# Attention kernel: row-max products in groups of two pairs over four PSUM banks, a unit's output joined in one bank, new order of jobs

## What is computed

```python
x = x + attn(layernorm(x))      # 16 heads of 64: q, k, v = x @ W.T
#   sim = q @ k.T * scale; e = exp(sim - max(sim)); out = (e / (sum(e) + 1e-10)) @ v; out @ Wo.T + bo
x = x + ffn(layernorm(x))       # blocks of 16 are rounded to an FP4 grid ahead of each product:
#   h = silu(x @ w_gate.T) * (x @ w_up.T); h @ w_down.T     (hidden width 352)
```

## Time and profile before

| | us |
|---|---|
| median of 3 runs (1461.32 to 1464.38) | 1464.04 |
| the profiled execution's own time | 1464.06 |
| its span | 1462.2 |
| TensorE busy | 1380.1 (94%) |
| VectorE, ScalarE, GpSimd busy | 1101.9 (75%), 1137.5 (78%), 1245.4 (85%) |

### The profile page before, as it was taken

How to read it: one execution, slowest core, us unless ns; L and a number is a source line. 1 busy time by engine, 2 the same in 40 slices (tenths; PEclk the granted TensorE clock), 3 DMA queues, 4 the chain that set the end, 5 groups by cost and what they waited for, 6 DMA issues and landing times.

```text
span 1462.2 us, 35256 instructions
## 1 busy us (share of the span) xinstructions
PE 1380.1 (94%) x13828; PEld 892.1 (61%) x13828; DVE 1101.9 (75%) x1717; ACT 1137.5 (78%) x2413; POOL 1245.4 (85%) x1391
## 2 busy tenths in 40 slices
PE   4899999998999999999999999999999999999965
PEld 2466665665666666666666666666666666666644
DVE  7767677677678878787887868788786878878567
ACT  3798888976888878788887878888787878878822
POOL 5798989987998988898898889899888989989932
PEclk8999999999999999999999999999999999999958
DMA  7111111111111102112111211211121121112000
GB/s 175 45 45 45 45 36 32 35 33 44 45 45 34 38 23 49 45 45 49 34 38 23 48 45 44 49 38 34 24 48 45 45 49 40 32 23 49 2 4 15
DMA packets 46660, 59.77 MB, mean 41 GB/s; under 512 B 8672, under 2 KB 21920, under 8 KB 46496
## 3 DMA queue, kind: packets, MB, share of 16 engines
q1 hardware_dynamic: 46336, 57.26, 16.8%
q10 hardware_dynamic: 160, 0.26, 0.1%
HBM read 4.80 MB, written 2.10 MB: 5 GB/s over the span
## 4 chain that ended last, share of the span: by engine, by line
PE 65%; DVE 20%; POOL 6%; ACT 5%; issue 3%; DMA 1%; SPq 0%; DVEq 0%
PE ob L635 16%; PE st L606 12%; PE st L608 10%; PE sm L587 8%; DVE negm L941 7%; POOL p_low L450 5%; PE mb L523 4%; PE mb L539 4%; PE mb L528 2%; PE mb L1242 2%; PE mb L534 2%; ACT probs L761 1%; DVE v L909 1%; DVE qv L1115 1%; DVE hidden L1119 1%
## 5 line engine op out<-in xcount | busy, mean ns | idle before, releaser
L450 POOL TENSOR_TENSOR p_low<-probs 128x512 f16<-128x512 f32 x1024 | 1083.0, 1076 | 148.2 <-ACT probs L761 145.1
L761 ACT ACTIVATE probs<-st,lift,exp_scale 128x512 f32<-128x512 f32 x1024 | 792.2, 779 | 172.4 <-PE st L608 159.9
L941 DVE TENSOR_REDUCE negm<-sm 128x1 f32<-128x1024 f32 x508 | 617.6, 1216 | 105.4 <-PE sm L587 104.2
L606 PE MATMUL st<-q_hl,k_hh 128*128 128x512 f16 x1024 | 394.7, 385 | 2.3 <-DMA q_hm<-m_low 2.3
L608 PE MATMUL st<-q_hm,k_l 128*128 128x512 f16 x1024 | 389.4, 380 | 0.0
L635 PEld LDWEIGHTS ob<-v,probs 128*128 128x128 bf16 x4096 | 279.3, 98 | 123.1 <-ACT oscl L775 1.0
L635 PE MATMUL ob<-v,probs 128*128 128x129 f16 x4096 | 322.4, 222 | 0.6 <-ACT oscl L775 0.5
L635 PEld LDWEIGHTS ob<-v,p_low 128*128 128x128 f16 x4096 | 195.7, 98 | 127.7 <-POOL p_low L450 8.7
L587 PE MATMUL sm<-k_hh,q_hl 64*128 64x512 f16 x508 | 197.5, 389 | 23.1 <-DVE negm L941 23.0
L635 PE MATMUL ob<-v,p_low 128*128 128x65 f16 x4096 | 211.2, 195 | 5.4 <-POOL p_low L450 5.3
L587 PE MATMUL sm<-k_hh,q_hm 64*128 64x512 f16 x508 | 197.7, 389 | 0.0
(11 more groups left out here) (175 smaller groups left out, 1539.1 us busy)
## 6 DMA issues: line engine op xcount, KB each, us to landing
k_hh<-k_high SPq DMA_DIRECT2D x128, 128.0 KB, 2.4
k_l<-k_low SPq DMA_DIRECT2D x64, 128.0 KB, 2.3
q_hl<-q_high SPq DMA_DIRECT2D x64, 128.0 KB, 2.3
q_hl<-q_low SPq DMA_DIRECT2D x64, 128.0 KB, 2.4
q_hm<-q_high SPq DMA_DIRECT2D x62, 128.0 KB, 2.3
x<-x SPq DMA_DIRECT2D x4, 512.0 KB, 7.3
q_hm<-m_high SPq DMA_DIRECT2D x128, 1.0 KB
q_hm<-m_low SPq DMA_DIRECT2D x128, 1.0 KB
```

The source lines that it names most:

```text
L450: return pool.tensor_tensor(p_low[b][:, j, :], p, p.bitcast(BF16)[:, 1::2], ALU.subtract)
L606: pe.matmul(st[s % 2][:, :], k_hh[n][:, s * P:(s + 1) * P], q_hl[n][:, half * HALF:(half + 1) * HALF], start=True, stop=False)
L761: nc.scalar.activation(probs[k % 2][:, s, :], st[s % 2][:, :], ACT.Exp, bias=lift[:, 0:1], scale=exp_scale[:, head, pair:pair + 1]).then_i ...
L941: nc.vector.tensor_reduce(negm[k % 2][:, s // 2:s // 2 + 1], banks[:, :, :].rearrange("p a n -> p (a n)"), AX.X, ALU.max, negate=True).the ...
```

## The change

`scores` is called in slots 0 and 4 and makes two pairs in a row: four matmuls in four banks. `sm` has four banks; its upper two serve jobs as well, as X0 and X1, beside one bank MB that only jobs use. A job in X0 or X1 waits until VectorE has reduced the group's first pair, and a group waits until the jobs ahead of it in X0 and X1 have been taken. VectorE reduces the first pair in slot 0 or 4 and the second in slot 1 or 5.

A unit's output (4 tiles x 65 columns) lies in the single bank `ob`. The high part is multiplied twice with the same probabilities, by 65 columns and by 64 that are added to the same place, so `join` on GpSimd falls away. The order within a unit is `VALUES`. ScalarE copies 260 columns out in slot 0 (`out_taken`), VectorE makes sums and reciprocals, and ScalarE scales 4 x 64 columns from SBUF in slots 3 and 4. `JOBS` has a new order. In the round ahead, `turn_rest` moves from slot (1, 1) to (3, 2), with the high and low parts behind it, and v0 waits for them; the DMA that ScalarE issues there moves from (1, 2) to (1, 3).

```diff
--- before.py
+++ after.py
...
...
-VC = 1 + 2 * DH
-VL = 1 + DH
-OT = 256
+VC = 1 + DH
...
-JOBS = [("k0", 0, (0, 1), (0, 2), (0, 2)), ("m", 1, (0, 1), (0, 2), (0, 2)), ("k1", 1, (0, 3), (0, 4), (0, 4)),
-        ("q0", 0, (0, 5), (0, 6), (0, 6)), ("t0", 0, (0, 7), (1, 0), None), ("m", 0, (1, 1), (1, 2), (1, 2)),
-        ("q1", 1, (1, 1), (1, 2), (1, 2)), ("o0", 0, (1, 3), None, (1, 4)), ("x", 0, (1, 5), (1, 6), None),
-        ("t1", 1, (1, 5), (1, 6), None), ("g0", 0, (1, 7), (2, 0), (2, 2)), ("h0", 0, (1, 7), (2, 0), None),
-        ("w2", 0, (1, 7), (2, 0), None), ("o1", 1, (1, 7), None, (2, 0)), ("m", 1, (2, 1), (2, 2), (2, 2)),
-        ("u0", 1, (2, 3), None, (2, 4)), ("h1", 1, (2, 3), (2, 4), None), ("w0", 1, (2, 3), (2, 4), None),
-        ("v0", 0, (2, 3), (2, 4), (2, 4)), ("g1", 0, (2, 7), (3, 0), (3, 2)), ("d", 0, (2, 7), None, (3, 0)),
-        ("n0", 0, (2, 7), (3, 0), (3, 0)), ("w1", 0, (2, 7), (3, 0), None), ("v1", 1, (2, 7), (3, 0), (3, 0)),
-        ("u1", 1, (3, 1), None, (3, 2)), ("m", 1, (3, 3), (3, 4), (3, 4)), ("n1", 0, (3, 3), (3, 4), (3, 4))]
+MB, X0, X1 = range(3)
+JOBS = [("m", X1, (0, 1), (0, 2), (0, 2)), ("k0", X0, (0, 1), (0, 2), (0, 2)), ("k1", MB, (0, 2), (0, 3), (0, 3)),
+        ("q0", X0, (0, 5), (0, 6), (0, 6)), ("t0", X1, (0, 6), (0, 7), None),
+        ("m", X1, (1, 1), (1, 2), (1, 2)), ("o0", X0, (1, 1), None, (1, 2)), ("q1", MB, (1, 2), (1, 3), (1, 3)),
+        ("t1", X0, (1, 5), (1, 6), None), ("x", MB, (1, 5), (1, 6), None),
+        ("g0", MB, (1, 7), (2, 0), (2, 2)), ("h0", MB, (1, 7), (2, 0), None), ("w2", MB, (1, 7), (2, 0), None),
+        ("m", X1, (2, 1), (2, 2), (2, 2)), ("o1", X0, (2, 1), None, (2, 2)),
+        ("h1", MB, (2, 3), (2, 4), None), ("w0", MB, (2, 3), (2, 4), None),
+        ("u0", X1, (2, 5), None, (2, 6)), ("n0", X0, (2, 5), (2, 6), (2, 6)),
+        ("g1", MB, (2, 7), (3, 0), (3, 2)), ("d", MB, (2, 6), None, (2, 7)), ("w1", MB, (2, 7), (3, 0), None),
+        ("m", X1, (3, 1), (3, 2), (3, 2)), ("u1", X0, (3, 1), None, (3, 2)), ("v0", MB, (3, 3), (3, 4), (3, 4)),
+        ("v1", X0, (3, 5), (3, 6), (3, 6)), ("n1", X1, (3, 5), (3, 6), (3, 6))]
...
+VALUES = {1: ((0, 0),), 2: ((0, 1),), 3: ((0, 2),), 4: ((1, 0),), 5: ((0, 3),), 6: ((1, 1),), 7: ((1, 2), (1, 3))}
...
+def has_max(r, k):
+
+    prev, cur, nxt = flags(r)
+    return cur if k < 2 else nxt
+
+
+def job_ahead(r, k, s, bank):
+
+    for back in range(2):
+        places = [(JOBS[m][ON_PE], m) for m in range(len(JOBS)) if r >= back and JOBS[m][1] == bank and runs(r - back, m)
+                  and (back or JOBS[m][ON_PE] < (k, s))]
+        if places:
+            place, m = max(places)
+            return m, back, (r - back, *place)
+    return None
+
+
+def maxima_ahead(r, k, s):
+
+    for back in range(r + 1):
+        for a in reversed(range(8)):
+            at = (a // 2, 4 * (a % 2))
+            if (back or at <= (k, s)) and has_max(r - back, at[0]):
+                return 4 * (4 * (r - back - 1) + at[0] + 2) + 2 * (a % 2), (r - back, *at)
+    return None
...
-        oscl = [sb(f"oscl{n}", [P, 2, 2 * DH]) for n in range(2)]
+        o_raw = [sb(f"o_raw{n}", [P, IT, VC]) for n in range(2)]
...
-        sm = psum("sm", [P, 2, 512])
-        sm_banks = [sm[:, n, :] for n in range(2)]
-        ob = [psum(f"ob{n}", [P, 512]) for n in range(2)]
-        mb = [psum(f"mb{n}", [P, 512]) for n in range(2)]
+        sm = psum("sm", [P, 4, 512])
+        sm_banks = [sm[:, n, :] for n in range(4)]
+        ob = psum("ob", [P, 512])
+        mb = [psum("mb", [P, 512]), sm_banks[2], sm_banks[3]]
 
...
-                        if s == 2 and (prev if k < 2 else cur):
-                            join(g, q, k, 1)
-                        if s == 6 and (prev if k < 1 else cur):
-                            join(g, q, k, 0)
...
-                pe.wait_ge(s_ks, 8)
+                pe.wait_ge(s_we, 2)
                 pe.wait_ge(s_ws[2], 1)
-                turn_w(2, 0, sm_banks[0])
-                turn_w(2, 1, sm_banks[1])
+                turn_w(2, 0, st[0])
+                turn_w(2, 1, st[1])
                 pe.wait_ge(s_ws[1], 1)
-                turn_w(1, 1, ob[0])
-                turn_w(0, 1, ob[1])
+                turn_w(1, 1, ob)
+                wait(pe, s_lo, 4)
+                turn_w(0, 1, mb[MB])
...
+                maxima = maxima_ahead(r, *JOBS[n][ON_PE]) if JOBS[n][1] != MB else None
+                if maxima is not None and (before is None or maxima[1] > (r - before[1], *JOBS[before[0]][ON_PE])):
+
+                    wait(pe, s_mx, maxima[0] + 1)
+                elif before is not None:
                     wait(pe, *taken(before[0], g - before[1]))
+                if r == 0 and name == "v0":
+
+                    pe.wait_ge(s_we, 6)
...
-                    pe.wait_ge(s_mx, 8)
...
-                    def scores(s):
+                    def scores(d):
 
                         n = 2 * q + 1 if k < 2 else 2 * (1 - q)
                         h = n % 2
-                        if k % 2 == 0 and s == 1:
+                        if k % 2 == 0 and d == 0:
                             wait(pe, s_dkh[h], 32 * (g + (1 if k else 0)))
                             wait(pe, s_dqh[h], 32 * (g + (1 if k else 0)))
-                        pair = 4 * (unit + 2) + s // 2
-                        if r == 0:
+                        earlier = maxima_ahead(r, k, 4 * d - 1)
+                        for bank in (X0, X1):
+                            last = job_ahead(r, k, 4 * d, bank)
+                            if last is not None and (earlier is None or last[2] >= earlier[1]):
+                                wait(pe, *taken(last[0], g - last[1]))
+                        for a in range(2):
+
+                            pair = 4 * (unit + 2) + 2 * d + a
                             wait(pe, s_mx, pair - 1)
-                        else:
-                            wait(pe, s_mx, pair)
-                        if r == 0 and pair == 1:
-
-                            pe.wait_ge(s_we, 6)
-                        banks = st_pair if r == 0 and pair % 2 == 0 else sm
-                        t = half * IT + s // 2
-                        for h, q_rows in enumerate((q_hl[n], q_hm[n])):
-                            rows = slice(h * DH, (h + 1) * DH)
-                            last = pe.matmul(banks[:, h, :], q_rows[rows, t * P:(t + 1) * P],
-                                             k_hh[n][rows, h * 512:(h + 1) * 512], start=True, stop=True)
-                        last.then_inc(s_sm, 2)
+                            t = half * IT + 2 * d + a
+                            for h, q_rows in enumerate((q_hl[n], q_hm[n])):
+                                rows = slice(h * DH, (h + 1) * DH)
+                                last = pe.matmul(sm_banks[2 * (1 - a) + h], q_rows[rows, t * P:(t + 1) * P],
+                                                 k_hh[n][rows, h * 512:(h + 1) * 512], start=True, stop=True)
+                            last.then_inc(s_sm, 2)
 
...
-                        if has_max and s % 2:
-                            scores(s)
+                        if has_max(r, k) and s % 4 == 0:
+                            scores(s // 4)
...
-                            bank, low, t = s // 4, s // 2 % 2, 2 * (s // 4) + s % 2
-                            if s % 4 == 0:
-
-                                wait(pe, s_ob, 2 * (unit - 1) + bank - 1)
-                            if k == 1 and s == 0:
-                                wait(pe, s_v, 2 * g)
-                            for j in range(JT):
-                                if s == 0 and j == 0:
-                                    wait(pe, s_ex, 8 * unit - 1)
-                                if s == 0 and j == JT - 1:
+                            for low, t in VALUES.get(s, ()):
+                                if (low, t) == (0, 0):
+
+                                    wait(pe, s_ob, unit - 1)
                                     wait(pe, s_ex, 8 * unit)
-                                if s == 2 and j == 0:
+                                    if k == 1:
+                                        wait(pe, s_v, 2 * g)
+                                if (low, t) == (1, 0):
 
                                     wait(pe, s_lp, JT * unit)
-                                if low:
-                                    p = p_low[1 - k % 2][:, j, t * P:(t + 1) * P]
-                                else:
+                                o = t * VC
+                                for j in range(JT):
+                                    v_j = v[pq][:, j, ph, :]
+                                    if low:
+                                        last = pe.matmul(ob[:, o:o + VC], p_low[1 - k % 2][:, j, t * P:(t + 1) * P],
+                                                         v_j[:, 1:1 + VC], start=False, stop=(j == JT - 1),
+                                                         skip_group_check=True)
```

(81 more changed lines are left out.)

52 lines of the change are left out of this document (21 added, 31 removed).

## The result

The changed kernel takes 1477.77 us (median of 9 runs, 1470.81 to 1483.67) against 1465.87 (1461.32 to 1467.06): ratio 1.0081, interval 1.0063 to 1.0099. I had said 1426 and 1402 to 1451. Its runs fall in two groups, four at 1470.8 to 1472.2 and five at 1477.8 to 1483.7; those of before do not. The profiled execution, 1471.7, is of the lower group.

The account below looks back on a forecast made before the run. It took TensorE's steps to bound the kernel, except near both ends, where GpSimd does. Terms of -50 + 16 - 5 - 5 + 5 + 1 = -38 on 1464.06 gave 1426 us, range 1402 to 1451.

Parts of the forecast that it names:

- Terms 1 and 2: TensorE: grouped pairs enter and leave the 64-row form once, -50 us; high value matmuls split in two, +16 us.
- Term 5: Round ahead: the moved turn_rest delays the first scores, +5 us, bounds 1 and 8.
- Term 4: GpSimd: 256 additions fall away, which counts only near the ends where the chain is GpSimd's, -5 us.
- the end: End of the kernel: the last output is copied whole, no half goes ahead; +1 us, between 0 and 2.
- ScalarE at nothing: ScalarE's new copy and scalings are covered by TensorE's own steps, 0 us; upper end 1 us a round, 32 in all.
- term 3: TensorE's waits for maxima: the old 23 us go, new waits cost 18; net -5 us, bounds -23 and +25.
- the waits' own bound: Upper bound of TensorE's new waits, all 8 groups late by 0.25 us: 48 in all, +30 on the sum.
- Costed at nothing: Side effects taken as 0 us: ScalarE's work, the single bank ob, the reciprocals' chain, and DMAs.
- the reciprocals' chain: Chain to the reciprocals within a unit: three hops longer but needed only in slots 3 and 4, 0 us.
- rival B: X banks: groups hold TensorE at their job or, with takes behind the second reduction, the next group; 1497 us, chance 0.09.
- The sign that the prediction named: Signs of error in TensorE's waits: L587 for x, k_low or q_low; jobs for negm over 30 us.
- Rivals A and C: A: second pairs pay losses again, 1451 (chance 0.05) or 1476 (0.01); C: strided value loads take 57 ns, 1639 (0.04).

Follow-up runs that it names:

- a_same: The changed kernel run again without any edit, as base for single edits; 1474.18 us, ratio 1.0075 to the kernel before.
- b_moves: The kernel before with only the moved VectorE steps of the quantisation of x and h; 1465.20 us against 1464.87, ratio 0.9999.
- a_scaled: The changed kernel with ScalarE's four scalings of a unit in slots 2 and 3 instead of 3 and 4; 1467.44 us, ratio 1.0025.
- c_den_act: The changed kernel with den made on ScalarE from o_raw instead of on VectorE, and one VectorE wait for its previous hidden added; 1453.08 us, ratio 0.9924.
- e_all_dve: d_all with den put back on VectorE; 1442.96 us, ratio 0.9843 to the kernel before.
- d_ts: c_den_act with the remaining weights turned at (1, 3) in round 0 and the scalings in slots 2 and 3; 1438.44 us, ratio 0.9820.
- d_x33: d_ts with VectorE's third step of the quantisation of x at (3, 3) instead of (3, 4); 1426.01 us, ratio 0.9732.
- d_all: d_x33 with the five later VectorE steps of the quantisation of h at other slots; 1416.68 us, ratio 0.9669.

## Why the prediction was wrong, point by point

**Terms 1 and 2, -50 and +16: right.** Pairs are 0.22 to 0.23 apart in fours, undoing it costs 69 with its waits, and a split costs 4 to 5 ns. TensorE from the first scores to the last exponential, and behind it, before and changed (columns as in the earlier trace rows):

```profile
39.60:1387.40 1347.80, 1318.52 (x13522) 849.16 (x13522) 1019.40 (x1542) 1104.43 (x2323) 1202.86 (x1336) 0.99 0.17 39
1387.40:1462.20 74.80, 44.45 (x218) 33.34 (x218) 52.12 (x108) 20.82 (x68) 23.40 (x25) 0.70 0.03 9
...
45.50:1400.80 1355.30, 1285.22 (x17576) 836.82 (x17575) 1025.91 (x1540) 1103.30 (x2194) 1099.22 (x1085) 0.99 0.17 39
1400.80:1469.90 69.10, 39.24 (x264) 29.15 (x260) 52.39 (x109) 21.54 (x68) 20.23 (x20) 0.76 0.04 10
```

In the rounds TensorE is busy for 33.3 us less, where the two terms had 34. **Term 5, +5: right:** the first exponential is at 46.57 instead of 40.64, +5.9 (45.7 in `a_same`).

**Term 4, -5, and the end, +1: the number fits, but in part by luck.** From the last exponential to the end of the span it is 69.1 us against 74.8, -5.7. That is not GpSimd's doing: `b_moves`, which still makes all 256 additions, has 69.8 there. TensorE idles about as long before and after (30.4 and 29.9); its granted clock was 0.70 in the kernel before, 0.76 in the changed one and 0.77 in `b_moves`. Why the clock differs there is open. What GpSimd gives is seen in less: its last low part ends 2.4 us behind the start of the last exponential instead of 4.6, and the first round is 1.3 shorter. It is busy for 1138.6, with no `o_n`.

**ScalarE at nothing, +0:** it is busy no more than before (1137.4 against 1137.5), but its place is not free: the scalings in slots 3 and 4 hold t1 at (1, 5), 0.42 us an even round (`a_scaled`).

What is left is TensorE's waits in the rounds: 1347.80 - 1318.52 = 29.3 before and 1355.30 - 1285.22 = 70.1 changed. That is +40.8, where terms 3 and 4 together had -10, and so 51 us of miss, of which the end hides some: -33.3 + 40.8 + 5.9 - 5.7 is, but for rounding, the +7.6 measured. The range was also added up wrongly at its upper end, since the waits' own bound, +30 on the sum, gives 1456 and not 1451; 1477.77 lies above both. Two steps failed.

First, **in "Costed at nothing", the reciprocals' chain** ("three hops longer but needed only in slots 3 and 4"). I asked who needs `rden`, not what stands behind `den` on its engine: the second reduction and all takes. Removing it gives 18.6 us (lower group against `c_den_act`), putting it back costs 26.3 in `e_all_dve`. Of the 18.6 the one long `den` is 7.0; most of the rest are the 1.0 us of each odd round, which go with L1110 running into a GpSimd instruction. The row that should have warned me is in the trace of before, VectorE, GpSimd and TensorE:

```profile
337.60 5.27 DVE L1089 TENSOR_SCALAR q_small<-q_small 128x22 f32<-128x22 f32 x1
...
335.38 3.04 POOL L450 TENSOR_TENSOR p_low<-probs 128x512 f16<-128x512 f32 x3
338.38 0.47 POOL L457 TENSOR_TENSOR o_n<-oscl 128x128 f32<-128x128 f32 x1
338.79 4.05 POOL L450 TENSOR_TENSOR p_low<-probs 128x512 f16<-128x512 f32 x4
...
345.15 0.61 PE L587 MATMUL sm<-k_hh,q_hl 64*128 64x512 f16 x1 [4.61 <-DVE negm L941]
```

It ends at 342.87, 0.03 behind GpSimd's row, and TensorE idles 4.61 us: the same event, once, in the 47.9 us round. `b_moves` has it twice (5.26 us at 337.55 and 4.68 at 1390.43). The change puts 128 more chances for it at the start of units. It also happens to undo this one: that row takes 0.52 us in the changed kernel and its round 42.2, so 5.7 us came back that nobody had forecast. The Trainium skill (SBUF — State Buffer, Who interferes with whom) says that a VectorE operation with two SBUF inputs, or `tensor_scalar` in its fast modes, contends with GpSimd for a shared port pair as a lock, and one SBUF input outside those modes does not. The rows here agree: 6.87 us for the `tensor_scalar` (that it ran in such a mode no row says) and 6.88 with two SBUF inputs, against 0.17 for the reciprocal and, by the times, none from PSUM. It speaks of waiting for one instruction, and 37 of 38 `den` did wait for just one; the other waited through a row of them, and what made it do so is open.

Second, **term 3's new waits, +18**. I priced half of the groups at 0.2 us. The mechanism was rival B's second half (the takes behind the second reduction), to which I gave 0.09: I took the reductions as back to back, when feed-forward steps at (0, 0), (0, 4), (1, 0) and (1, 4) stand between them. Moving the steps gives 21.8 us. The scalings, with `o_n` needed at (1, 5), give most of 9.3: `d_ts` less its 5.3 at the front. 18.6 + 21.8 + 9.3 = 49.7 is about the 51 by which the waits missed. In the rounds TensorE's waits go from 70.1 to 52.3 (`c_den_act`), 48.8 (`d_ts`), 39.2 (`d_x33`) and 31.3 us (`d_all`). That is still above the 29.3 of the kernel before and the 19 of the forecast, so that `d_all` has its rounds does not make term 3 right: it is another placement. The sign that the prediction named for this, the groups' matmuls waiting for x, `k_low` or `q_low`, came true; the other, jobs waiting for `negm` for over 30 us, did not.

Rivals A and C fell at once (pairs 0.23 apart, even rounds 0.7 us shorter).

## What to carry over

When an operation is moved to another engine, price it by everything queued behind it there, however small it is, and look in the trace for the longest of its kind, not the mean: one 5.27 us row among 27 named the risk. Reductions in a row are one block only if no other work is placed between them; after regrouping, walk each slot of the old placement again. And if several waits lie in one round, single edits show a fraction of their worth (0.33 of 1.44 us); stack them before judging.

## What was new about the hardware

A VectorE operation on 4 columns from SBUF that ran into a GpSimd instruction ended 23 to 31 ns behind that instruction's end, 37 times of 38 in the changed kernel; the other time it waited 6.87 us through six adjacent ones, and in another form 6.88. When it does the one and when the other is open. A stall of 4 to 5 us costs more than itself: the granted clock fell to 0.50 and stayed there for about 4 us of work, and the round with 5.35 us of idle time was 7.0 longer. A matmul of 64 columns with its own 128 x 128 load goes by every 29 to 33 ns, so splitting one of 129 columns costs 4 to 5 ns; a kernel that has waits shows less of it (8.6 us for 4096). A group of matmuls on 64 rows loses 0.10 us on entry and 0.09 to 0.11 on leaving once, however many follow (four here); the Trainium skill (TensorEngine Tiling (Array Packing), Key Properties) says that changing the tiling mode drains the engine, and these are its prices in this kernel.
